# Blocks of dummy matmuls added behind four more stages of an adaLN transformer layer on eight cores

## What is computed

```python
mod = (silu(c) @ wmod)                     # six vectors: sa, ca, ga, sb, cb, gb
h = layernorm(x) * (1 + ca) + sa
q, k, v = h @ Wq.T + bq, h @ Wk.T + bk, h @ Wv.T + bv      # rotary on q and k
qp, kp = [sin, cos] of R @ (q/|q|), R @ (k/|k|)
out = einsum(qp, einsum(kp, v))            # linear attention over the heads
x = x + ga * (out @ Wo.T + bo)
h = layernorm(x) * (1 + cb) + sb
x = x + gb * (routed_experts(h) + shared_expert(h))
```

## Time and profile before

| | us |
|---|---|
| runs of the kernel | 3871.19, 3936.62, 4017.9 (median 3936.62) |
| the profiled execution, its own time | 3888.02 |
| its span on core 0, the slowest | 3886.4 |
| spans of the eight cores | 3826.1 to 3886.4 |
| mean granted TensorE clock of the cores | 0.797 to 0.805 of full speed |
| PE busy, core 0 | 2575.2 (66%) |

### The profile page before, as it was taken

One profiled execution on the slowest core, in us unless ns is written; L12 is line 12 of the kernel. 1 busy time (PEld: TensorE's weight loads), 2 busy tenths in 40 slices (PEclk: granted clock), 3 DMA queues, 4 the chain that ended last, 5 costly groups with the idle time before them and its releaser, 6 DMA issues.

```text
span 3886.4 us, 32735 instructions; the slowest of 8 cores (3826.1 to 3886.4 us)
## 1 busy us (share of the span) xinstructions
PE 2575.2 (66%) x11048; PEld 1108.1 (29%) x11048; DVE 1355.2 (35%) x2504; ACT 379.4 (10%) x422; POOL 171.1 (4%) x294
## 2 busy tenths in 40 slices
PE   3359732334972333593399579986899589976886
PEld 1124311112431111231144233432344234432332
DVE  0466265655623454536422022221222022211203
ACT  0121212121111101102100000000000000000000
POOL 0000000000000111000000000000000000000000
PEclk8569855556986555795599889998899789987998
DMA  9514410000435534710153765448543864457547
GB/s 164 115 44 66 68 28 25 17 25 3 66 52 84 100 68 76 174 23 0 37 95 66 162 232 108 92 87 234 161 92 65 191 221 91 92 118 218 165 76 268
DMA packets 84942, 395.13 MB, mean 102 GB/s; under 512 B 7184, under 2 KB 7440, under 8 KB 75312
## 3 DMA queue, kind: packets, MB, share of 16 engines
q0 software_dynamic: 41536, 208.26, 31.2%
q1 hardware_dynamic: 33696, 146.98, 11.0%
q10 hardware_dynamic: 9552, 37.80, 2.8%
HBM read 538.26 MB, written 46.20 MB: 150 GB/s over the span
## 4 chain that ended last, share of the span: by engine, by line
PE 51%; DMA 24%; DVE 13%; issue 7%; ACT 3%; DVEq 0%; POOL 0%; ACTq 0%; POOLq 0%; SPq 0%
PE pb L1055 23%; PE pb L618 9%; PE pb L1131 8%; DMA AW<-wmod 8%; DMA AW<-w2i 5%; DMA AW<-w2scr 4%; PE pb L923 3%; DMA AW<-w1i 3%; DMA w2scr<-AW 2%; DVE AMS L786 2%; PE pb L429 2%; DVE AMS L1143 2%; PE pb L578 2%; DVE AHT L583 1%; DVE AMS L789 1%
## 5 line engine op out<-in xcount | busy, mean ns | idle before, releaser
L1055 PE MATMUL pb<-AHT,AW 128*128 128x512 bf16 x4608 | 1007.8, 381 | 63.7 <-DMA AW<-w1i 49.7
L1131 PE MATMUL pb<-AW,AOT 128*128 128x512 bf16 x2304 | 590.6, 422 | 286.5 <-DMA AW<-w2i 156.8
L1055 PEld LDWEIGHTS pb<-AHT,AW 128*128 128x128 bf16 x4608 | 450.9, 98 | 620.5 <-issue 89.2
L1131 PEld LDWEIGHTS pb<-AW,AOT 128*128 128x128 bf16 x2304 | 241.1, 106 | 636.0 <-issue 425.9
L618 PE MATMUL pb<-AW,AHT 128*128 128x512 bf16 x1536 | 352.9, 383 | 0.0
L1143 DVE TENSOR_TENSOR AMS<-pb,AMS 128x2048 f32<-128x2048 f32 x40 | 91.7, 2292 | 721.3 <-PE pb L1131 719.2
L578 PE MATMUL pb<-identf,AX 128*128 128x128 f32 x256 | 98.8, 444 | 279.3 <-ACT AX L539 240.0
L429 PE MATMUL pb<-AW,scol 128*1 128x512 bf16 x384 | 137.8, 537 | 140.8 <-DMA AW<-wmod 129.4
L1079 ACT ACTIVATE AMS<-AMS 128x1024 f32<-128x1024 f32 x64 | 67.6, 1056 | 1466.0 <-DVE AMS L1076 1466.0
L1081 DVE TENSOR_TENSOR AMS<-pb,AMS 128x1024 f32<-128x1024 f32 x64 | 78.4, 1224 | 368.7 <-PE pb L1055 368.7
L618 PEld LDWEIGHTS pb<-AW,AHT 128*128 128x128 bf16 x1536 | 143.6, 98 | 183.7 <-issue 27.7
(11 more groups left out here) (150 smaller groups left out, 1754.0 us busy)
## 6 DMA issues: line engine op xcount, KB each, us to landing
AW<-w2scr SPq DMA_DIRECT2D x54, 2048.0 KB, 9.2
AW<-wmod POOLq DMA_DIRECT2D x24, 2048.0 KB, 19.8
w2scr<-AW ACTq DMA_DIRECT2D x18, 2048.0 KB
AW<-w1i POOLq DMA_DIRECT2D x32, 1024.0 KB, 8.2
AW<-w3i POOLq DMA_DIRECT2D x32, 1024.0 KB, 8.6
AW<-w2i POOLq DMA_DIRECT2D x16, 2048.0 KB, 23.2
AX<-xin SPq DMA_DIRECT2D x16, 1024.0 KB, 5.9
AW<-wqt POOLq DMA_DIRECT2D x4, 2048.0 KB, 17.8
```

The lines of the kernel that those rows point to most:

```text
L1055: ins = tt.matmul(pu[:, th * 512:(th + 1) * 512], slot(sl)[:, ic * 128:(ic + 1) * 128], ahtb[:, ic * 1024 + th * 512: ic * 1024 + (th + 1) ...
L1131: ins = tt.matmul(pw[:, ob * 512:(ob + 1) * 512], hebuf[:, hc * 1024 + tau * 128: hc * 1024 + tau * 128 + 128], slot(ws)[:, ob * 512:(ob + ...
```

## The change

`emit_warm(n)`, n matmuls of the 128x128 identity with 512 columns of the cosine table into bank 0 of `pb0`, is defined earlier, with the same text, and called at four more places. Nothing is removed; the block of stage 4 stays as it is.

```diff
+        def emit_warm(n):
+            def wfn(tt):
+                for _ in range(n):
+                    ins = tt.matmul(pb0[:, 0:512], identb[:], cosbuf[:, 0:512],
+                                    start=True, stop=True)
+                return ins
+            sch.op("tensor", wfn, reads=["identb", "cosbuf"],
+                   writes=W(ar_p0, "warm", 0, 2048))
+
         for t in range(8):
             emit_ln1_tile(0, t, True, None, lnxsA, ...)
+            emit_warm(20)
...
             emit_mod_jb(8 + 2 * t)
             emit_mod_jb(9 + 2 * t)
+            emit_warm(16)
         emit_wo_wdma(1)
         emit_mid_B(1, 7)
...
             if ob + 2 < 4:
                 emit_wo_wdma(ob + 2)
+            emit_warm(12)
...
             ln_tile(x1t(t), [f"x1_{t}"], lnxsB, ...)
             transpose_h_tile(t, lnxsB, cbcol, sbcol, ["col4", "col3"])
+            emit_warm(16)
```

More of the change, by code:

```diff
@@ L839, in _build @@
         emit_qkv_wdma(1)
[L841 to L848, removed]
         for t in range(8):
```

## The result

| | before | changed |
|---|---|---|
| median of all runs, us | 3883.76 (10 runs) | 3940.00 (8 runs) |
| profiled execution, us | 3888.02 | 3939.92 |
| spans of the eight cores, us | 3826.1 to 3886.4 | 3887.7 to 3938.3 |
| mean granted clock of the cores | 0.797 to 0.805 | 0.812 to 0.819 |

The ratio of the runs is 1.0162, with a 95% interval of 1.0141 to 1.0183: 63 us on 3884. The forecast was +17.7. 3940 us lies inside the range of the time, but that range was as wide as it was because of the scatter between single runs; the effect's own range, 0 to +24 us, was missed.

The account below looks back on a forecast made before the run. PE was taken to bound the output projection but idle in LN1, LN2 and stage 6 pauses. 4.6 + 8.7 + 5.4 - 1 = +17.7 us gave 3905.7 by the profile, 3954.3 by the median, middle 3930; range 3878 to 4028, effect 0 to +24.

Parts of the forecast that it names:

- The change, part by part: Step pricing the 464 added matmuls place by place in LN1, stage 6, output projection and LN2; total +17.7 us.
- The last paragraph: Signs to check in the changed kernel, such as a projection of about 135 us, and what would show the forecast wrong.
- LN1, last block, with proj. 1: Block 8 of LN1, hidden by nothing, delays the first projection but absorbs its slow start: net +4.6 us.
- output projection: First three of four blocks of 12 stand between PE-bound groups and cost +8.7 us; the fourth costs 0.
- gate: LN2's block 8 stands before the gate's first matmuls: 5.1 us plus 0.3 for an eviction, +5.4 us.
- The drain: In the output projection, the next group writes bank 0 and waits for the block to drain: 0.16 us each.
- The cover of stage 6: Stage 6's 8 blocks of 16, at most 6.9 us each, end before L795, which waits for DVE: 0.
- The gain from the clock: One faster round of two transposes after each of LN1's blocks 1 to 7, 0.12 us each, about -1 us; LN2 none.
- A: Clock stays up through LN1 and LN2 bursts, 112 rounds shorten by 13 us: +5 us, 3893 by the profile; chance 0.17.
- B: Hidden blocks slow DVE and ACT in the pauses: slower by over 2%; chance 0.04 shared with D in full.
- C: Later waits on transfers absorb the delays, nothing is exposed: time as before, 3888 by the profile; chance 0.06.
- D: Pauses do not cover the blocks, all 464 matmuls exposed: 106 us; chance 0.03 in part, 0.04 in full with B.

Follow-up runs that it names:

- after_best: Changed kernel with the waits ordered own counter first, then transfers', GpSimd's, ScalarE's, TensorE's, VectorE's; ratio to before 1.0037.
- before_best: Kernel before, no new block, waits ordered own counter first, then transfers', GpSimd's, ScalarE's, TensorE's, VectorE's; ratio to before 0.9993.
- The crossed kernels: Kernels before and changed, each with TensorE's or VectorE's counter first (before_tv, before_vt, after_tv, after_vt); profiled 3887.6, 3906.3, 3907.2, 3960.9 us.
- after_big: Changed kernel in the wait order of before_best, blocks of 40 in LN1, stage 6 and LN2, 24 in the output projection; profiled 3964.0 us.
- before_tv: Kernel before with waits in a fixed order, ScalarE's, TensorE's, VectorE's, GpSimd's counters, then the transfers'; ratio to before 1.0021.
- after_tv: Changed kernel with the fixed wait order of before_tv, TensorE's counter ahead of VectorE's; ratio to before 1.0087.
- after_vt: Changed kernel with a fixed wait order, VectorE's counter ahead of TensorE's; ratio to before 1.0177.
- before_vt: Kernel before, no new block, with a fixed wait order, VectorE's counter ahead of TensorE's; profiled 3906.3 us.
- before_pruned: before_best where a writer skips waiting for a buffer's last writer if readers stand between, 765 fewer waits on TensorE's queue; ratio to before 0.9963.
- tuned: before_pruned with blocks of 28 behind tiles 1 to 7 of LN1 and LN2, 72 ahead of stage 4's transpose bursts, none elsewhere; ratio to before 0.9971.
- after_hidden: Changed kernel in before_best's wait order without LN1's and LN2's eighth blocks and the output projection's first three; ratio to before 0.9966.
- after_again: Text of the changed kernel, unchanged, built once more; profiled 3936.0 us.
- after_line: Changed kernel with three lines of comment at the head of the file; profiled 3916.0 us.
- only_wo: Kernel before with one of the four new calls, the block of 12 behind each part of the output projection; profiled 3894.1 us.

## Why the prediction missed

**Which stages grow.** The stage differences sum to 54.1 us. Blocks, by after_best against before_best: 15.8. Order of waits: what is left of LN1 (10.8 - 4.0 = 6.8), stage 4 (14.3), LN2 (2.9 + 1.5 = 4.4) and the gate (0.9), and of stage 6 the 7.6 us of the table below, 34.0 us in all. The crossed kernels show it for LN1, stage 4, LN2 and the gate.

Stage 6 becomes clear when the time is taken out in which TensorE stands idle ahead of L429 until a transfer of modulation weights (`wmod`) has landed. That time differs from core to core and from execution to execution, and it hides the rest. In us, means over the eight cores:

| kernel | blocks in stage 6 | stage 6 | idle for `wmod` | rest |
|---|---|---|---|---|
| before_best | none | 450.3 | 56.0 | 394.3 |
| after_best | 16 | 455.4 | 60.1 | 395.3 |
| after_big | 40 | 449.9 | 54.9 | 395.0 |
| before | none | 457.7 | 55.3 | 402.4 |
| before_tv | none | 466.8 | 58.5 | 408.4 |
| changed | 16 | 471.9 | 61.9 | 410.0 |
| after_tv | 16 | 467.4 | 56.7 | 410.8 |
| after_vt | 16 | 475.3 | 61.5 | 413.8 |
| before_vt | none | 465.9 | 51.7 | 414.2 |

The rest goes by the order of waits, not by the blocks: 394 to 395 us with the blocking wait last (395.2 in before_pruned, but 399.2 in tuned), 414 with VectorE's counter ahead of TensorE's. From before to the changed kernel it grew by 7.6 us, and the idle time for transfers by 6.6. Kernels with blocks of 16 wait somewhat longer for `wmod` (55.3 to 62.1 us, with after_hidden, after_again and after_line) than those without (50.6 to 58.5), the one with blocks of 40 does not; a cause is not shown.

Of the 54.1 us 4.3 are left, 1.8 in stage 6 (9.4 by the medians, less 7.6) and 2.5 in stages whose code is alike. The measured ratio asks for 63 us, 11 more than the profiled executions; one such pair does not fix a difference of 11, since the text of before, built again, was profiled at 3867.9 instead of 3888.0. The experts, the stage that follows the gate, stay open: they took 1934 to 1944 us in six of the eight kernels with exposed blocks, but 1933.1 in after_tv and 1929.8 in only_wo, and 1926.8 to 1934.8 in the kernels without.

**The step that failed.** Under "The change, part by part" the sum held only the 464 matmuls: everything else of the program, the waits that the scheduler generates included, was taken to stay as it was, a term of nothing without a reason. The runs showed some 34 us there: a met wait behind the blocking one, 0.106 us a time, in LN1, stages 4 and 6 and LN2. The sentence was that the pauses "keep their places: a tile every 17.5 us"; tiles came every 18.1 (first transposes at 153.35 to 262.20, six tiles on). The last paragraph came nearest, with "if the stages between 1941 us and the end changed length by more than the exposed blocks explain", but it looked only behind the last block, where nothing but the experts lies, and not at stages 4 and 6; and no rival had a mechanism for it. That the order could move stood in the code, where `_emit_waits` sorts by `id`; which way it would move, and so the 34 us, could not be read there. Its price, 0.106 us, stood in no row that I had read; it can be read only from the records of PE's sequencer, and what decides is how often it is paid: once a round in every burst of transposes.

**The terms of the sum.**

| term | predicted | measured |
|---|---|---|
| LN1, last block, with proj. 1 | +4.6 | +4.5 (after_best - after_hidden: 6.9 - 2.4) |
| LN1, 7 covered blocks, with proj. 1 | -1 | -2.5 (after_hidden - before_best: -2.9 + 0.4) |
| output projection | +8.7 | +9.4 (after_best - before_best) |
| LN2, 7 covered blocks | 0 | -1.5 (the same) |
| gate | +5.4 | +5.9 (the same) |
| sum | +17.7 | +15.8 |
| stage 6, 8 blocks | 0 | +1.0; with blocks of 40, +0.7 (the rest, in the table above) |

The part of the sum that was written down was right to 2 us. The exposed blocks and their drain can be read on core 0 of the changed kernel, with the earlier trace rows as their counterpart:

```profile
271.08 6.10 PE L819 MATMUL pb<-cosbuf,identb 128*128 128x512 bf16 x20
277.44 2.75 PE L618 MATMUL pb<-AW,AHT 128*128 128x512 bf16 x12 [0.26 <-PE pb L819]
...
1705.68 2.76 PE L819 MATMUL pb<-cosbuf,identb 128*128 128x512 bf16 x12
1708.70 1.67 PE L924 MATMUL pb<-AW,AMS 128*128 128x512 bf16 x7 [0.26 <-PE pb L819]
...
1926.47 5.25 PE L819 MATMUL pb<-cosbuf,identb 128*128 128x512 bf16 x16 [0.19 <-PE pb L548]
1931.56 0.55 PE L965 MATMUL pb<-AW,AHT 128*128 128x8 bf16 x16
```

6.10 us for 20 (6.0 predicted), 5.25 for 16 (5.1), and the first L618 starts fast. In the projection 12 matmuls and the drain take 1708.70 - 1705.68 = 3.02 us against 2.9. The drain itself was predicted at 0.16 us and is 0.15 where no other wait stands behind TensorE's own; the 0.26 and 0.37 of most groups are the same omitted term, met waits behind the blocking one.

**The cover of stage 6** held. In one tile of the changed kernel the block ends and PE idles 4.91 us more until DVE has done its part.

```profile
1329.65 5.01 PE L819 MATMUL pb<-cosbuf,identb 128*128 128x512 bf16 x16
1339.57 0.26 PE L795 MATMUL pb<-AMS 128*128 128x128 bf16 x1 [4.91 <-DVE AMS L789]
```

**The gain from the clock** was underrated: on average 2.4 short rounds per burst in LN1 where one was predicted, 0.7 in LN2 where none was, and 0.14 us each where 0.12 was taken. The count began at the mean time that the clock stayed up, 3.6 us, out of a spread of 2.2 to 4.8. In the burst of after_tv above the block ended at 149.58 and the granted clock was still 1.00 in 153 to 154 us and 0.52 in 154 to 155, some 4.5 us later.

**The rivals.** A, a clock that stays up through the bursts, was wrong as told: it fell in each burst. B, contention in the pauses, is refuted: on the eight cores the 120 reductions that ran beside a block took 2.276 us on average, the 72 others 2.277, and those of before 2.28. On core 0:

```profile
L511 DVE TENSOR_REDUCE lns<-AX 128x1 f32<-128x2048 f32 x24 | 54.6, 2276 | 0.0
```

C and D did not occur: the exposed blocks cost 4.5 + 9.4 + 5.9 = 19.8 us in their stages, and PE's waits behind blocks 1 to 7 of LN1 ended with ACT as before. The chance of 0.70 for the forecast was too high for a kernel whose program is generated: none of the cases held a change in the generated order. That 3940 us lies inside the range of the time all the same is luck: the scatter between runs made that range wide, not the effect.

## What to carry to other kernels

Where each wait is an instruction of its own, put the wait that blocks last: a met wait ahead of it costs nothing that these runs show, one behind it costs about 0.11 us on TensorE each time, here up to 21 us in one stage (stage 4: 492.5 to 513.5). A scheduler must not sort by object addresses. Two versions are comparable only when their order of waits is fixed; where it is not, the unchanged text built again and a version with nothing but a comment added should be timed before a difference of under 2% is explained. Dummy matmuls are worth their place only inside a pause that ends soon behind them: behind a mean of 2.4 us a burst had 2.4 short rounds on average (after_hidden, LN1), behind 3.4 to 6.5 us it had none or one (tuned, stage 4). At the end of a stage, or between two stretches bound by TensorE, they cost their full 0.23 us each.

## What the runs showed of the hardware

- A met wait behind a blocking one on TensorE's sequencer takes 0.106 us (503.529 to 503.635); the round of two transposes and two evictions grew from 1.11 to 1.22 us. Behind a block of dummy matmuls the idle time is 0.15, 0.26 and 0.37 us with none, one and two met waits behind the blocking one.
- A round of two float32 transposes and their evictions takes 0.97 us at the high clock, 1.11 at the low one, with the blocking wait last.
- Transposes ran at the high clock when a block had raised it (0 to 4 short rounds per burst of LN1 in after_hidden, 3 to 5 in after_big), but a burst of them neither raised it (none in the 56 bursts of before_best) nor kept it.
- DVE's reduction of 128x2048 float32 takes the same 2.276 us with dummy matmuls beside it as without.
